# A gated cross-attention block: three buffers for the values, one query table, and the spills and top rows at other places of the DMA queue

## The reference

```python
x = x + tanh(g_xattn) * xattn(layernorm(x), ctx, ctx, 0, mask)
x = x + tanh(g_ffn)   * ffn(layernorm(x), ...)
```

## Time and profile before

| | |
|---|---|
| median of 3 runs | 1156.43 us (1155.88 to 1156.44) |
| the profiled execution | 1153.81 us |
| its span, first to last instruction | 1152.0 us |
| mean granted TensorE clock | 0.990 |
| PE busy | 1071.3 us (93%) |
| POOL busy | 865.2 us (75%) |
| ACT busy | 891.2 us (77%) |
| DVE busy | 864.8 us (75%) |
| moved by DMA | 95.56 MB, 83 GB/s on average |

### The profile page before, as it was taken

One profiled execution on the slowest core, in us unless ns is written; L12 is line 12 of the kernel. 1 busy time (PEld: TensorE's weight loads), 2 busy tenths in 40 slices (PEclk: granted clock), 3 DMA queues, 4 the chain that ended last, 5 costly groups with the idle time before them and its releaser, 6 DMA issues.

```text
span 1152.0 us, 42802 instructions
## 1 busy us (share of the span) xinstructions
PE 1071.3 (93%) x18241; PEld 775.3 (67%) x18276; DVE 864.8 (75%) x2134; ACT 891.2 (77%) x1159; POOL 865.2 (75%) x600
## 2 busy tenths in 40 slices
PE   4998989898999999899999998899979999999998
PEld 2776767677677777677767776777767655555554
DVE  4877877777788778677777887778854899676776
ACT  3999979998899899789989988999961444655554
POOL 5999989999998999889989989999961110423424
PEclk9999999999999999899999999999989999999999
DMA  9322233223223222332233131123135500012214
GB/s 338 114 81 70 57 71 81 76 59 91 70 57 78 80 71 56 71 88 70 62 88 89 46 71 43 47 54 77 43 141 150 212 1 1 1 50 98 111 76 180
DMA packets 102588, 95.56 MB, mean 83 GB/s; under 512 B 84481, under 2 KB 85505, under 8 KB 98562
## 3 DMA queue, kind: packets, MB, share of 16 engines
q1 hardware_dynamic: 101682, 91.79, 27.8%
q10 hardware_dynamic: 720, 1.05, 0.2%
HBM read 71.75 MB, written 20.97 MB: 80 GB/s over the span
## 4 chain that ended last, share of the span: by engine, by line
PE 42%; POOL 29%; issue 13%; ACT 12%; DVE 2%; DMA 1%; SPq 1%; POOLq 0%; DVEq 0%; ACTq 0%
POOL arena L587 20%; PE psum L1005 12%; PE psum L949 7%; ACT arena L748 7%; PE psum L936 5%; POOL arena L547 4%; ACT arena L752 4%; PE psum L981 3%; PE psum L1091 3%; PE psum L969 2%; PE psum L970 2%; PE psum L992 2%; POOL arena L614 1%; ACT arena L723 1%; PE psum L1130 1%
## 5 line engine op out<-in xcount | busy, mean ns | idle before, releaser
L587 POOL TENSOR_TENSOR arena<-arena 128x1536 bf16<-128x1536 f32 x224 | 614.5, 2749 | 16.9 <-ACT arena L748 15.9
L1361 DVE CUSTOM_DVE_ANT_0 arena<-psum,arena 128x750 f32<-128x750 f32 x448 | 407.7, 938 | 152.5 <-PE psum L936 116.1
L748 ACT ACTIVATE arena<-psum 128x768 f32<-128x768 f32 x448 | 363.4, 811 | 82.6 <-POOL arena L587 42.7
L752 ACT ACTIVATE arena<-arena,neg_max 128x750 f32<-128x750 f32 x448 | 409.7, 915 | 4.4 <-DVE neg_max L1361 4.4
L949 PE MATMUL psum<-ident,arena 64*128 64x64 f32 x5376 | 265.6, 231 | 53.4 <-ACT arena L748 49.4
L949 PEld LDWEIGHTS psum<-ident,arena 64*128 64x128 f32 x5376 | 210.9, 140 | 125.9 <-issue 116.9
L936 PE MATMUL psum<-arena 64*128 64x512 bf16 (+1 forms) x2688 | 262.3, 327 | 3.8 <-DVE neg_max L1361 2.2
L970 PE MATMUL psum<-arena 128*128 128x64 bf16 (+1 forms) x2688 | 198.0, 194 | 1.4 <-issue 1.4
L969 PE MATMUL psum<-arena 128*128 128x65 bf16 (+1 forms) x2688 | 198.8, 195 | 0.1
L936 PEld LDWEIGHTS psum<-arena 64*128 64x128 bf16 x2688 | 124.4, 95 | 93.7 <-issue 9.4
L970 PEld LDWEIGHTS psum<-arena 128*128 128x128 bf16 (+1 forms) x2688 | 176.9, 99 | 1.7 <-issue 1.7
(11 more groups left out here) (167 smaller groups left out, 1068.1 us busy)
## 6 DMA issues: line engine op xcount, KB each, us to landing
arena<-in_k_t SPq DMA_DIRECT2D x128, 187.5 KB, 3.2
arena<-in_v_rows SPq DMA_DIRECT2D x64, 192.0 KB, 3.4
out<-arena SPq DMA_DIRECT2D x10, 1024.0 KB, 3.9
arena<-in_x_top SPq DMA_DIRECT2D x8, 1024.0 KB, 6.0
arena<-in_x_rest SPq DMA_DIRECT2D x8, 768.0 KB, 6.1
spill<-arena SPq DMA_DIRECT2D x96, 64.0 KB, 2.2
arena<-spill SPq DMA_DIRECT2D x6, 1024.0 KB, 11.0
arena<-in_w_t SPq DMA_DIRECT2D x4, 1024.0 KB, 15.2
```

The costliest lines, as they stand in the source:

```text
L587: pool.tensor_tensor(p_lo[:, slots, :], p_sb[:, slots, :], high(p_sb[:, slots, :]), ALU.subtract).then_inc(p_split, 1)
L748: act.activation(p_sb[:, n % RING, :].rearrange("p (c h q) -> p h c q", h=2, q=HALF), turned_ps, ACT.Copy).then_inc(evac_a, 1)
L752: act.activation(s_sb[:, n % RING, 0:CTX], s_sb[:, n % RING, 0:CTX], ACT.Exp, bias=neg_max[:, n % 4, :], scale=-1.0).then_inc(exped, 1)
L1361: dve.tensor_tensor_reduce(s_sb[:, n % RING, 0:CTX], flat_ps[:, score_at(s):score_at(s) + CTX], mask_sb[:, max(m - REP + 1, 0), :], -1.0, ...
```

## The change

It does five things.
1. `v_raw` gets three slots, by g % 3, with three load counters. v(2) is loaded in the prologue, v(2 * both + 2) at the start of a double group (once the values of the group that had its slot are done), and v(2 * both + 3) in its middle.
2. `split_v` waits on POOL for the values of group g - 2, whose low halves lie in the slot of `v_lo` that it writes (there are still two).
3. `q_hi` and `q_lo` become a single table each.
4. The spill of a batch is issued in two halves of six DMAs, in the first and in the second double group of the next batch.
5. The top rows of batch b + 2 are loaded in the fourth double group of batch b, no longer in the second.

In the arena `k_lo` moves behind `xb`, and a gap has another size.

```diff
@@ -165,13 +165,13 @@
         xn_rest = carve("attention", [128, KV, NB, D])
         k_raw = carve("attention", [128, 2, CTX])
         p_lo = carve("attention", [128, RING, CW], BF16)
-        v_raw = carve("attention", [128, 2, NCH, D + 1])
+        v_raw = carve("attention", [128, 3, NCH, D + 1])
         v_lo = carve("attention", [128, 2, NCH, D], BF16)
+        carve("attention", [128, 188])
+        xb = carve("attention", [128, 3, NB, KV * D])
         k_lo = carve("attention", [128, 2, CTX], BF16)
-        carve("attention", [128, 250])
-        xb = carve("attention", [128, 3, NB, KV * D])
-        q_hi = carve("attention", [128, 2, UNITS, 128], BF16)
-        q_lo = carve("attention", [128, 2, UNITS, 128], BF16)
+        q_hi = carve("attention", [128, UNITS, 128], BF16)
+        q_lo = carve("attention", [128, UNITS, 128], BF16)
 
         h_rows = carve("ffn", [128, 2, 512])
         h_hi = carve("ffn", [128, 4, 4, 128], BF16)
@@ -239,7 +239,7 @@
         top_second = sem("top_second")
         spilled = [sem(f"spilled{i}") for i in range(3)]
         k_loaded = [sem("k_loaded0"), sem("k_loaded1")]
-        v_loaded = [sem("v_loaded0"), sem("v_loaded1")]
+        v_loaded = [sem(f"v_loaded{i}") for i in range(3)]
         k_split = sem("k_split")
         v_split = sem("v_split")
         q_turned = sem("q_turned")
@@ -396,7 +396,7 @@
                     sp.dma_start(k_raw[D * part:D * part + D, g % 2, :], k_t[g]).then_inc(k_loaded[g % 2], 16)
 
             def load_v(g):
-                sp.dma_start(v_raw[:, g % 2, :, 0:D], v_rows[g].rearrange("p (c d) -> p c d", c=NCH)).then_inc(v_loaded[g % 2], 16)
+                sp.dma_start(v_raw[:, g % 3, :, 0:D], v_rows[g].rearrange("p (c d) -> p c d", c=NCH)).then_inc(v_loaded[g % 3], 16)
 
             def gather_rest(b):
                 sp.wait_ge(rest_summed, b + 1)
@@ -408,9 +408,9 @@
                 for r in range(REP):
                     sp.dma_start(ln_mv[QUAD * r:QUAD * r + QUAD, 1:1 + NB, :], mv_rest[:]).then_inc(rest_spread, 16)
 
-            def spill_rest(b):
+            def spill_rest(b, quads=range(REP)):
                 sp.wait_ge(x_added, KV * (b + 1))
-                for r in range(REP):
+                for r in quads:
                     for j in range(NB):
                         at = b * REST + j * QUAD
                         sp.dma_start(spill[at:at + QUAD].rearrange("i (g r d) -> i g r d", g=KV, r=REP)[:, :, r, :],
@@ -424,6 +424,7 @@
             sp.dma_start(mask_sb[:, 1:1 + NB, :], mask[:, 1:1 + NB, :]).then_inc(mask_rest_loaded, 16)
             load_k(1)
             load_v(1)
+            load_v(2)
             load_top(1)
             load_rest(1)
             for i in range(4):
@@ -439,26 +440,28 @@
                 if both + 1 < PAIRS:
                     sp.wait_ge(scored, 2 * UNITS * both + UNITS + 1)
                     load_k(2 * both + 2)
-                if both > 0:
+                if 0 < both and both + 1 < PAIRS:
                     sp.wait_ge(valued, 2 * UNITS * both)
-                    load_v(2 * both + 1)
+                    load_v(2 * both + 2)
                 if at == 2 and b + 1 < BATCH:
                     spread_rest(b + 1)
                 if both + 1 < PAIRS:
                     sp.wait_ge(scored, 2 * UNITS * (both + 1))
                     load_k(2 * both + 3)
                     sp.wait_ge(valued, 2 * UNITS * both + UNITS)
-                    load_v(2 * both + 2)
+                    load_v(2 * both + 3)
                 if at == 0 and b > 0:
-                    spill_rest(b - 1)
+                    spill_rest(b - 1, range(0, 2))
                 if at == 0 and b + 1 < BATCH:
                     gather_rest(b + 1)
-                if at == 1 and b + 2 < BATCH:
-                    load_top(b + 2)
+                if at == 1 and b > 0:
+                    spill_rest(b - 1, range(2, REP))
                 if at == 2 and b + 2 < BATCH:
                     if b >= 1:
                         sp.wait_ge(spilled[(b + 2) % 3], 16 * REP * NB * ((b - 1) // 3 + 1))
                     load_rest(b + 2)
+                if at == 3 and b + 2 < BATCH:
+                    load_top(b + 2)
 
             def load_piece(i):
                 slot = i % STAGE_SLOTS
@@ -548,8 +551,10 @@
                                    ALU.subtract).then_inc(k_split, 1)
 
             def split_v(g):
-                pool.wait_ge(v_loaded[g % 2], 16 * (g // 2 + 1))
-                pool.tensor_tensor(v_lo[:, g % 2], v_raw[:, g % 2, :, 0:D], high(v_raw[:, g % 2, :, 0:D]), ALU.subtract).then_inc(v_split, 1)
+                pool.wait_ge(v_loaded[g % 3], 16 * (g // 3 + 1))
+                if g >= 2:
+                    pool.wait_ge(valued, UNITS * (g - 1))
+                pool.tensor_tensor(v_lo[:, g % 2], v_raw[:, g % 3, :, 0:D], high(v_raw[:, g % 3, :, 0:D]), ALU.subtract).then_inc(v_split, 1)
 
             steps = [0]
 
@@ -737,7 +742,7 @@
             def round_first(i):
                 turns = FIRST_TURNS[i]
                 act.wait_ge(q_turned, i + 1)
-                act.activation(q_hi[:, 0, turns[0]:turns[-1] + 1, :],
+                act.activation(q_hi[:, turns[0]:turns[-1] + 1, :],
                                mix_ps[:, FIRST_BANK[i], 0:128 * len(turns)].rearrange("p (t n) -> p t n", n=128),
                                ACT.Copy).then_inc(q_hi_done, 1)
 
@@ -933,7 +938,7 @@
                             u = groups[s] % 2
                             q = q_lo if term == 1 else q_hi
                             kk = k_lo[rows, u, cols] if term == 2 else high(k_raw[rows, u, cols])
-                            mm = pe.matmul(flat_ps[:, score_at(s) + cols.start:score_at(s) + cols.stop], q[rows, both % 2, p, :], kk,
+                            mm = pe.matmul(flat_ps[:, score_at(s) + cols.start:score_at(s) + cols.stop], q[rows, p, :], kk,
                                            start=(term == 0), stop=(term == 2))
                 mm.then_inc(scored, 2)
 
@@ -966,7 +971,7 @@
                     for c in range(NCH):
                         rows = chunk_rows(c)
                         hi = high(p_sb[0:rows, n % RING, c * 128:(c + 1) * 128])
-                        pe.matmul(o, hi, high(v_raw[0:rows, u, c, :]), start=(fresh and c == 0), stop=False, skip_group_check=True)
+                        pe.matmul(o, hi, high(v_raw[0:rows, g % 3, c, :]), start=(fresh and c == 0), stop=False, skip_group_check=True)
                         pe.matmul(o[:, 0:D], hi, v_lo[0:rows, u, c, :], start=False, stop=False, skip_group_check=True)
 
             def value_low(j):
@@ -978,7 +983,7 @@
                     for c in range(NCH):
                         rows = chunk_rows(c)
                         lo = p_lo[0:rows, n % RING, c * 128:(c + 1) * 128]
-                        mm = pe.matmul(mix_ps[:, g % 2, at:at + D + 1], lo, high(v_raw[0:rows, g % 2, c, :]), start=False, stop=(c == NCH - 1),
+                        mm = pe.matmul(mix_ps[:, g % 2, at:at + D + 1], lo, high(v_raw[0:rows, g % 3, c, :]), start=False, stop=(c == NCH - 1),
                                        skip_group_check=True)
                     mm.then_inc(valued, 1)
 
@@ -1232,22 +1237,22 @@
                     ins = dve.bn_aggr(mv_rest[:, j, :], gathered[:, j, :, :])
                 ins.then_inc(rest_merged, 1)
 
-            def low_q(both, turns, bank):
+            def low_q(turns, bank):
                 cols = slice(turns[0], turns[-1] + 1)
-                dve.tensor_tensor(q_lo[:, both % 2, cols, :], mix_ps[:, bank, 0:128 * len(turns)].rearrange("p (t n) -> p t n", n=128),
-                                  q_hi[:, both % 2, cols, :], ALU.subtract).then_inc(q_split, 1)
+                dve.tensor_tensor(q_lo[:, cols, :], mix_ps[:, bank, 0:128 * len(turns)].rearrange("p (t n) -> p t n", n=128),
+                                  q_hi[:, cols, :], ALU.subtract).then_inc(q_split, 1)
 
             def split_first(i):
                 dve.wait_ge(q_hi_done, i + 1)
-                low_q(0, FIRST_TURNS[i], FIRST_BANK[i])
+                low_q(FIRST_TURNS[i], FIRST_BANK[i])
 
             def split_q(both, part):
                 turns, bank = part_turns(part), part_bank(part)
                 dve.wait_ge(q_turned, parts_split(both, part))
-                dve.tensor_copy(q_hi[:, both % 2, turns[0]:turns[-1] + 1, :],
+                dve.tensor_copy(q_hi[:, turns[0]:turns[-1] + 1, :],
                                 mix_ps[:, bank, 0:128 * len(turns)].rearrange("p (t n) -> p t n", n=128)).then_inc(q_hi_own, 1)
                 dve.wait_ge(q_hi_own, 2 * (both - 1) + part + 1)
-                low_q(both, turns, bank)
+                low_q(turns, bank)
 
             for c in range(4):
                 top_stats(0, c)
```

## The result

The changed kernel took 1129.55 us in the median of four runs (1128.4 to 1130.73), against 1156.43 us of the kernel before; the ratio is 0.9764, with a 95% interval of 0.9748 to 0.9781. Forecast was 1129.0, in a range of 1124 to 1137. The profiled execution took 1128.4 us with a span of 1126.6, which is 25.4 us less than the span before. The difference of the medians is 26.9 us; the profiled execution before was 2.6 us under its median, the one after 1.2 us.

A forecast was written before the change was run, and what follows sets the result against it. PE with ACT set a floor per double group, POOL being the limit in 2 to 10; only 40.7 us of excess could go. Terms -21.3 - 5.8 - 0.8 + 0.5 = -27.4 us took the 1156.4 median to 1129.0, range 1124 to 1137.

The forecast's parts named there:

- The floor: Attention part: PE with ACT need 24.36 us per double group, 25.95 in those with three more ACT normalizations.
- POOL's room under it: Double groups 11 to 31: POOL's own 23.44 us lies 0.9 us under the floor; waits cost only what exceeds that.
- rival A: Value waits on POOL: the whole 37.1 us of waiting comes back, giving 1119 us; chance 5%.
- Double groups 11 to 30: Of 23.1 us above the floor, 21.3 are gained as every value wait at L552 goes.
- the four with the layer norm's factors: Double groups 14, 18, 22, 26, with factors on POOL: each stays 0.46 us above the floor, 1.8 in all.
- Double groups 2 to 10: POOL, also making low halves of w1 or wq, is the limit; gain 5.8 us, at most 6.3.
- the two long ones: Double groups 3 and 7, ACT's long ones: POOL may catch up and idle, so the low end is 4.
- +0.5 for v(2): Prologue: 192 KB more ahead of k(2), for which POOL already waits 1.46 us; cost 0.5 us, between 0 and 1.1.
- -0.8 for the value wait: Double groups 0 and 1: POOL waits 1.0 us for values; gain 0.8 us, between 0 and 1.0.
- The added wait: POOL, ahead of a value split: the preceding low-half subtraction already waited for the same count; cost 0.
- POOL beside VectorE: Skill rule against the change: denser POOL work would lengthen; at 10 ns per L587, 2.2 us, most under the floor.
- The clock: PE's granted clock, 0.50 after a 4.66 us POOL wait before, should stay at 1.00 up to 840 us.

The follow-up runs named there:

- The kernel with one added split: The changed kernel with one more, unneeded value split on POOL (0.78 us) in each of double groups 11 to 30; 1133.63 us.
- v(2) behind k(2): The changed kernel with v(2) loaded in the loop behind k(2), no longer in the prologue; 1127.69 us, ratio 0.9754.
- w1 behind it too: The changed kernel with v(2) behind k(2) and all four w1 pieces at the end of double group 0's loads; 1124.95 us, ratio 0.9721.
- the spread w1: The changed kernel with v(2) behind k(2) and one w1 piece in each of the first four double groups; 1124.58 us, ratio 0.9738.

## Why the prediction was right

The sum was -27.4 us; measured were -26.9 in the medians and -25.4 in the profiled spans. The sum was worked out in the trace, so the second is its measure, and it was 2.0 us too high. That the median came within 0.6 us of 1129.0 is in part luck: the two profiled executions lay 2.6 and 1.2 us under their medians.

1. **The floor.** It was said that no double group can take less than 24.36 or 25.95 us, and that POOL's room under it is 0.9 us. The kernel after has 24.4 to 24.5 and 26.0 in nearly all of double groups 11 to 30. The two kernels with added POOL work show the room from the other side: 0.78 us per double group is nearly free, a further 0.78 is not. Of the 37.1 us of waits 36.1 lay in double groups 2 to 30, and they were worth 28.1 us. The room is why they were not worth more, and why rival A had no place to come from.
2. **Double groups 11 to 30.** -21.3 forecast, -21.4 measured, though from other parts. I kept 0.46 us in each of the four with the layer norm's factors, and they have only 0.06 to 0.3. The rows of the kernel before would have told it: number 14 holds a value wait of 0.45 us,

```profile
400.27 0.83 POOL L552 TENSOR_TENSOR arena<-arena 128x384 bf16<-128x384 f32 x1 [0.45 <-DMA arena<-in_v_rows]
```

and numbers 18, 22 and 26 hold waits of 1.69, 1.47 and 1.17 us, where they stood 1.69, 1.48 and 1.17 above the floor. With the factors POOL has no room in them, a wait passes through in full, and it went with the change. The kernel with one added split agrees: what its 0.78 us cost, 0.4 to 0.9 us each, it cost in these four. Against that nearly all twenty are up to 0.1 us longer than my floor, which is mostly the addresses' doing and to which I had given 0.
3. **Double groups 2 to 10.** -5.8 forecast, -6.7 measured. It was right that POOL is the limit here and that the waits pass through in full; I took less than the row's 6.3 us for fear of the two long ones, where POOL turned out to idle for nothing. The 6.3 that I called the most was passed by 0.4 us, which no row explains.
4. **The start.** This is the term that was mis-sized: +0.5 for v(2) and -0.8 for the value wait, against +3.0 us measured. The step that failed was to take POOL's wait of 1.46 us for k(2) as a property of the kernel. With the same DMAs in the prologue it was 1.4 us in one profile and 3.6 in another, and with v(2) among them up to 4.1. Behind a wait of over 3 us PE's clock fell in six of nine executions, with double group 0 at 27.84 to 29.97 us; in three, with waits of 3.23, 3.58 and 3.98 us, it stayed at 1.00, and double group 0 took 26.72 to 27.45. All nine executions with w1 ahead and the queue at its lower rate waited for over 3 us (in the kernel with the buffers alone the profile names PE for the 3.75 us), the two at the higher rate for 1.4 to 1.5. Against the single table alone, whose first two double groups took 53.4 us, the kernel after lost nothing at the start. v(2)'s own share was not isolated: at the lower rate, kernels with it ahead waited for 3.1 to 4.1 us and kernels without it for 3.2 to 3.6.
5. **The added wait, the query table, the spills and the top rows** at 0: the runs with each alone or taken away agree, as far as 1 us can be told. But the spills were not priced as what they are, a second remedy for the same loss. The prediction laid the whole gain to the buffers; the spills alone bring five sixths of it in the medians and seven tenths by the marks of double groups 2 to 30.
6. **POOL beside VectorE.** I weighed a rule of the Trainium skill (GPSIMD Engine Reference, Key points), that POOL shares its SBUF interfaces with VectorE and contends with some of VectorE's instructions. L592 lasts 2750 ns in the mean, as L587 did to within 1 ns, with POOL's waits for values gone. The trace does not show the contention in this kernel.
7. **The clock.** It was to stay at 1.00 up to 840 us. From 50 us on it does, at 0.99 to 1.00; in the window from 42 to 46 us it was 0.74.

## What to carry to other kernels

Sum up a wait's worth from the distance between the stage's period and the next engine's floor, not from the idle time: here 0.9 us in each plain period was free, nothing where POOL had extra work, and 36 us of idle time were worth 28. Where a load is late because of what stands ahead of it in a queue and because its slot is free too late, either remedy alone may bring most of it, so try each alone before paying for both. Look at what bulk loads stand ahead of the first pieces that an engine waits for: 4 MB that are needed 55 us later cost 2.7 to 4.4 us here in the medians (from v(2) behind k(2) to w1 behind it too, and from the kernel after to the spread w1).

Take a second profile of the same kernel before a wait of one trace goes into a sum.

## What the runs showed of the hardware that was not expected

- With the same DMAs in the prologue the queue moved 402 and 408 GB/s between 16 and 24 us in two executions, and 345 to 355 in three; POOL's first wait for the DMA queue was 1.4 and 1.5 us in the two and 3.2 to 3.6 in the three. What sets the rate is open.
- Behind a wait of over 3 us on POOL at the start PE's granted clock fell in some executions and not in others: with 3.21 us it was 0.74 from 42 to 46 us, part of the time at its lower level of 1.2 GHz, with PE busy for 1.59 us of 4; with 3.23 us it was 1.00, with PE busy for 1.77. With a wait of 1.46 us it stayed at 2.4 GHz.
- Moving buffers in SBUF, with no instruction added or taken away, lengthened a double group that PE and ACT set from 24.36 to 24.43 us.
